# Retention output of a Perceiver block as three one-pass products, its weights split on GpSimd

## The reference

```
x = x + cross_attention(layernorm(x), context)           # 16 heads of 16, masked keys
n = layernorm(x)
q, k, v, g = n @ Wq.T, n @ Wk.T, n @ Wv.T, n @ Wg.T      # retention: 4 heads, q and k 64 wide, v and g 128
q, k = rotary(q), rotary(k)
o = ((q k^T / 8) * decay) @ v                            # causal, decay gamma^(i-j) for each head
o = o * rsqrt(mean(o*o) + 1e-5) * gnorm_w * silu(g)
x = x + o.reshape(256, 512) @ Wo.T                       # "retention output"
m = layernorm(x)
w = softmax(m @ gate_w + gate_b); w = w * (w >= 0.1); w = w / sum(w)
x = x + sum_e w[:, e] * (m @ expert_w[e] + expert_b[e])  # 8 experts
```

## Time and profile before

| | |
|---|---|
| median of 3 runs | 205.86 us (205.49 to 207.44) |
| profiled execution | 204.96 us, span 203.1 us |
| TensorE busy | 193.9 us, 95% of the span, 2446 matmuls |
| VectorE busy | 140.0 us, 69%, 269 instructions |
| ScalarE busy | 108.2 us, 53% |
| GpSimd busy | 74.7 us, 37%, 96 instructions |
| mean granted TensorE clock | 0.995 |

### The profile page before, as it was taken

One profiled execution on the slowest core, in us unless ns is written; L12 is line 12 of the kernel. 1 busy time (PEld: TensorE's weight loads), 2 busy tenths in 40 slices (PEclk: granted clock), 3 DMA queues, 4 the chain that ended last, 5 costly groups with the idle time before them and its releaser, 6 DMA issues.

```text
span 203.1 us, 5924 instructions
## 1 busy us (share of the span) xinstructions
PE 193.9 (95%) x2446; PEld 134.5 (66%) x2446; DVE 140.0 (69%) x269; ACT 108.2 (53%) x230; POOL 74.7 (37%) x96
## 2 busy tenths in 40 slices
PE   8998999989999999999999999999999999999991
PEld 8566654555576767666666656476777888878780
DVE  3482568997388286688888627289676485996893
ACT  3136575759588386788888996244416333201200
POOL 8506695556191241079998331001003013010000
PEclk9999999999999999999999999999999999999998
DMA  5969966338209679066000000000000000000011
GB/s 165 299 189 258 329 161 162 90 85 230 50 5 241 135 207 362 20 217 204 5 5 5 3 0 3 0 3 0 0 0 2 3 0 2 0 5 26 26 32 36
DMA packets 15828, 18.10 MB, mean 89 GB/s; under 512 B 2657, under 2 KB 14897, under 8 KB 15793
## 3 DMA queue, kind: packets, MB, share of 16 engines
q1 hardware_dynamic: 14496, 17.30, 29.1%
q10 hardware_dynamic: 1296, 0.34, 0.8%
HBM read 9.81 MB, written 0.52 MB: 51 GB/s over the span
## 4 chain that ended last, share of the span: by engine, by line
PE 79%; DVE 8%; SPq 4%; ACT 3%; issue 2%; DMA 1%; POOL 0%; DVEq 0%; ACTq 0%; POOLq 0%
PE bank L919 11%; PE bank L1014 11%; PE bank L996 11%; PE bank L876 5%; PE bank L862 4%; DVE cneg L1849 4%; PE bank L1214 3%; PE bank L1064 3%; PE bank L1103 3%; PE bank L1238 3%; PE bank L1107 3%; PE bank L1240 3%; PE bank L1239 3%; PE bank L809 3%; PE bank L1104 3%
## 5 line engine op out<-in xcount | busy, mean ns | idle before, releaser
L1849 DVE TENSOR_REDUCE cneg<-bank 128x1 f32<-128x896 f32 x64 | 67.9, 1088 | 25.1 <-PE bank L919 24.8
L1526 ACT ACTIVATE prob<-bank 128x512 f32<-128x512 f32 x112 | 64.3, 600 | 13.2 <-PE bank L996 11.8
L996 PE MATMUL bank<-qstack,kstack 100*32 100x256 bf16 x896 | 45.0, 273 | 0.8 <-ACT prob L1526 0.5
L919 PE MATMUL bank<-kstack,qstack 97*32 97x448 bf16 x512 | 37.5, 354 | 1.6 <-DVE cneg L1849 0.9
L996 PEld LDWEIGHTS bank<-qstack,kstack 100*32 100x32 bf16 x896 | 24.4, 95 | 18.9 <-ACT prob L1526 4.1
L1014 PE MATMUL bank<-prob,vals 128*32 128x256 f32 x448 | 35.6, 381 | 0.0
L604 POOL TENSOR_TENSOR nw<-nw,halves 128x2 f32<-128x2 f32 (+1 forms) x10 | 8.3, 825 | 63.6 <-DVE nw L1730 45.1
L919 PEld LDWEIGHTS bank<-kstack,qstack 97*32 97x32 bf16 x512 | 13.6, 96 | 7.7 <-DVE cneg L1849 3.5
L1014 PEld LDWEIGHTS bank<-prob,vals 128*32 128x32 f32 x448 | 13.5, 109 | 4.5 <-issue 2.9
L1238 PE MATMUL bank<-exp_high,xn_high 128*128 128x512 f32 (+1 forms) x36 | 14.3, 397 | 0.0
L2095 DVE SCALAR_TENSOR_TENSOR x_in<-bank,nwts,x_in 128x256 f32<-128x256 f32 x28 | 13.5, 482 | 0.8
(11 more groups left out here) (186 smaller groups left out, 322.1 us busy)
## 6 DMA issues: line engine op xcount, KB each, us to landing
kstack<-kpart SPq DMA_DIRECT2D x21, 224.0 KB
w_late<-in_w_ret SPq DMA_DIRECT2D x1, 1536.0 KB, 8.7
mask_all<-in_mask SPq DMA_DIRECT2D x2, 512.0 KB, 4.5
ctxT<-in_w_exp SPq DMA_DIRECT2D x1, 1024.0 KB, 5.3
kpart<-in_w_exp SPq DMA_DIRECT2D x1, 1024.0 KB, 8.9
ctxT<-in_ctxT SPq DMA_DIRECT2D x2, 448.0 KB, 5.0
ctxT<-in_ctxT SPq DMA_DIRECT2D x1, 896.0 KB, 7.9
qstack<-acc SPq DMA_DIRECT2D x12, 64.0 KB, 4.1
```

Of the source, the lines that this page charges most:

```text
L919: mm = pe.matmul(out[j4:j4 + COLS, :], qstack[0:MROW + 1, h, b, qt * P + j4:qt * P + j4 + COLS], kstack[0:MROW + 1, b, h, half_ * HC:(half ...
L996: mm = pe.matmul(out[j4:j4 + COLS, hh * NQ:(hh + 1) * NQ], kstack[0:KROWS, b, h, kt * P + j4:kt * P + j4 + COLS], qstack[0:KROWS, h, b, :] ...
L1526: act.activation(prob[:, n % PROBS, :], bank[:, c.score_bank(u, jj), :], ACT.Exp).then_inc(c["prob_ready"], 1)
L1849: dve.tensor_reduce(cneg[:, st % 2, i:i + 1], bank[:, pair:pair + 2, 0:HC], AXXY, ALU.max, negate=True).then_inc(c["max_read"], 1)
```

## The change

`retention_out` becomes split products. A tile has 12 one-pass matmuls in place of 4 float32 ones: y_high x reto_high and y_high x reto_low, and, once DVE has written the low part, y_low x reto_high. ScalarE's copy writes `y_high` (rounded) and counts on `high_taken`; DVE's new `take_low_y` computes y_low = bank x norm weights - y_high, 128x512, four times. In the first batch these stand after each of the first two decay weights, in the second batch before and after the second of the weight parts' calls. GpSimd cuts `w_reto` in `late_roots`, after the roots of the first two streams, when the second batch's stream is normalised (`n2_ready`): one copy and one subtraction of 128x1024. `y_high` and `reto_high` lie where the second batch's keys were, `y_low` in the room of `y_tok`. `high_taken` now counts y as well, so its waits are indexed by a list. The first batch's biases go one pair of experts later on TensorE, and one step later on DVE.

```
@@ gpsimd, late_roots
                     root(NB + n, width, first)
+                    if n == 1:
+                        pool.wait_ge(s["n2_ready"], TT)
+                        pool.tensor_copy(reto_high[:, :, :], w_reto[:, :, :]).then_inc(s["split"], 1)
+                        pool.wait_ge(s["split"], SPLIT_ALL + 1)
+                        pool.tensor_tensor(reto_low[:, :, :], w_reto[:, :, :], reto_high[:, :, :].bitcast(F32), ALU.subtract).then_inc(s["split"], 1)
+                        pool.wait_ge(s["split"], SPLIT_OUT)
@@ tensor
                 def retention_out(t):
-                    taken("y", t)
+                    pe.wait_ge(s["split"], SPLIT_OUT)
+                    pe.wait_ge(s["high_taken"], HIGH_AT["y", t] + 1)
                     pe.wait_ge(s["rope_read"], TT)
                     out = side("ro", t)
                     for c in range(4):
-                        mm = pe.matmul(out[:, 0:D], yT[:, c, t * P:(t + 1) * P], w_reto[:, c, :], start=(c == 0), stop=(c == 3))
+                        pe.matmul(out[:, 0:D], y_high[:, c, t * P:(t + 1) * P], reto_high[:, c, :], start=(c == 0), stop=False)
+                        pe.matmul(out[:, 0:D], y_high[:, c, t * P:(t + 1) * P], reto_low[:, c, :], start=False, stop=False)
+                    taken("y", t)
+                    for c in range(4):
+                        mm = pe.matmul(out[:, 0:D], y_low[:, t, c, :], reto_high[:, c, :], start=False, stop=(c == 3))
                     mm.then_inc(s["side_ready"], 1)
...
                 pair(1, 0)
+                pair(1, 1)
                 biases(0)
-                pair(1, 1)
                 pair(1, 2)
@@ scalar
                 def take_y(t):
-                    take_turn("y", t, yT[:, :, t * P:(t + 1) * P], bank[:, turn_bank("y", t), :].rearrange("p (f q) -> p f q", f=4), scale=gn[:, 0:1])
+                    assert TURNS[len(takes)] == ("y", t)
+                    act.wait_ge(s["turned"], len(takes) + 1)
+                    act.activation(y_high[:, :, t * P:(t + 1) * P], bank[:, turn_bank("y", t), :].rearrange("p (f q) -> p f q", f=4), ACT.Copy,
+                                   scale=gn[:, 0:1]).then_inc(s["high_taken"], 1)
+                    takes.append(("y", t))
@@ vector
+            def take_low_y(t):
+
+                dve.wait_ge(s["high_taken"], HIGH_AT["y", t] + 1)
+                dve.scalar_tensor_tensor(y_low[:, t, :, :], bank[:, turn_bank("y", t), :].rearrange("p (f q) -> p f q", f=4), gn[:, 0:1],
+                                         y_high[:, :, t * P:(t + 1) * P].bitcast(F32), ALU.mult, ALU.subtract).then_inc(s["turn_taken"], 1)
...
                 decay_weights(RH)
+                take_low_y(0)
                 decay_weights(RH + 1)
+                take_low_y(1)
                 second_stream(0, [lambda: decay_weights(RH + 2)])
...
                 gate_weights(0)
+                take_low_y(2)
                 weight_parts(0)
+                take_low_y(3)
                 add_experts(0, range(0, 6))
                 second_stream(1, [lambda e=e: add_experts(1, [e]) for e in (0, 1)], lambda: add_experts(0, range(6, NE)))
+                add_experts(1, range(2, 4))
                 add_biases(0)
-                add_experts(1, range(2, 4))
                 take_low("n3", 2)
```

More of the change, by code:

```diff
@@ L137 @@
 SPLIT_ALL = 14
+SPLIT_OUT = 16
+KSTACK_BYTES = NB * NH * CH * 2
 PER = {"k_ready": 8, "k_hi": 4, "k_rest": 4, "k_taken": 4, "k_mid": 4, "k_cut": 4, "v_ready": NVP + 2, "v_evac": NVP + 2,
@@ L156 @@
 TURN_AT = {what: n for n, what in enumerate(TURNS)}
+HIGH_AT = {what: n for n, what in enumerate(what for what in TURNS if what[0] in ("n2", "n3", "y"))}
 SIDE_AT = {what: n for n, what in enumerate(SIDES)}
@@ L379, in build @@
         xn_low = sb_over("k_full", 0, "xn_low", [P, KIN, TT * P])
+        reto_high = sb_over("kstack", KSTACK_BYTES - 4 * NV * D // P, "reto_high", [P, NV // P, D])
+        reto_low = sb_over("w_late", 4 * ret_cols, "reto_low", [P, NV // P, D])
+        y_high = sb_over("kstack", KSTACK_BYTES // NB + 4 * 2048, "y_high", [P, NV // P, TT * P])
+        y_low = sb_over("vals", 4 * 1024, "y_low", [P, TT, NV // P, P])
         late0 = qstack[:, :, :, :].rearrange("p h b q -> p (h b q)").bitcast(F32)
@@ L390, in build @@
         qkT = late1[:, 0:4 * TT * P].rearrange("p (f t) -> p f t", f=4)
-        yT = late1[:, 2048:4096].rearrange("p (f t) -> p f t", f=4)
         qk_rot = late1[:, 4096:5120].rearrange("p (t c) -> p t c", t=2)
@@ L1096, in project_ret @@
             def project_ret(t, m, halves=(0, 1)):
-                pe.wait_ge(s["high_taken"], t + 1)
+                pe.wait_ge(s["high_taken"], HIGH_AT["n2", t] + 1)
                 if t:
@@ L1949, in take_low @@
             def take_low(kind, t):
-                n = t + 1 + (TT if kind == "n3" else 0)
-                dve.wait_ge(s["high_taken"], n)
+                dve.wait_ge(s["high_taken"], HIGH_AT[kind, t] + 1)
                 dve.tensor_tensor(xn_low[:, :, t * P:(t + 1) * P], bank[:, turn_bank(kind, t), 0:D].rearrange("p (f q) -> p f q", f=KIN),
                                   xn_high[:, :, t * P:(t + 1) * P].bitcast(F32), ALU.subtract).then_inc(s["turn_taken"], 1)
+            def take_low_y(t):
+                dve.wait_ge(s["high_taken"], HIGH_AT["y", t] + 1)
+                dve.scalar_tensor_tensor(y_low[:, t, :, :], bank[:, turn_bank("y", t), :].rearrange("p (f q) -> p f q", f=4), gn[:, 0:1],
+                                         y_high[:, :, t * P:(t + 1) * P].bitcast(F32), ALU.mult, ALU.subtract).then_inc(s["turn_taken"], 1)
             def first_stream(b):
```

## The result

The changed kernel takes 209.09 us (median of four runs, 207.38 to 210.41) against 205.9 for the kernel before. The ratio is 1.015, with a 95% interval of 1.0077 to 1.0223. The forecast was 208.2 with a range of 205.3 to 209.0, so the sign and the mechanism held, and the median lies 0.09 over the range.

The account below looks back on a forecast made before the run. TensorE, busy 95% of the span, was taken as the bound, with DVE also short of slack in the second batch. Terms -0.61 + 0.81 + 2.1 = +2.3 us gave 208.2 us against the 205.86 median, range 205.3 to 209.0.

Parts of the forecast that it names:

- The products: Retention output on TensorE: one-pass matmuls save 0.61 us per two-tile batch, 1.22 in all; first batch keeps its gain.
- The second batch: Two new DVE instructions add 1.38 us without slack; TensorE's second 0.61 saving goes and gate logits start 0.81 us late.
- The two waits: Second batch: TensorE waits before the third n3 tile's transpose and before its logits, each 0.6 to 0.8 us.
- The biases: First batch's bias product one pair later on TensorE: costs nothing, waiting under 0.1 us instead of over 1 us.
- GpSimd's split: After the second stream is normalised: GpSimd's subtraction starts 0.3 us before DVE's rotation, costing between 0 and 2.1 us.
- the upper end: At DVE's first rotation: it starts only when GpSimd's subtraction is over, a loss of 2.1 us; taken for the forecast.
- The rival of full speed: Rotation loses nothing beside GpSimd's subtraction, or DVE comes first: +0.2 us, 206.1; chance 0.30.
- sharing: At the rotation, DVE is slowed beside GpSimd, not stopped: half of 2.1 us, +1.25 in all, 207.1; chance 0.12.
- the rival of the hidden DVE work: Second batch's low parts take under 0.57 us, logits not late, no rotation loss: 205.25 or 204.6; chance 0.07.
- the products are not one pass: Retention output matmuls run at the old 0.217 us, 1.7 us more in the first batch: 209.7; chance 0.03.
- The sum: Whole kernel: -0.61 first batch, +0.81 second batch, +2.1 rotation, giving +2.3 us and 208.2 us.
- no clock effect enters: Retention output stretches: granted clock is 1.00 in both, the 2.4 GHz level, so no time was added for it.

Follow-up runs that it names:

- the reordered kernel: Changed kernel with GpSimd's copy and subtraction held until the third tile is rotated, plus DVE's second-batch expert sums in another order; 205.2 us, ratio 0.9954.
- the two halves: Changed kernel with GpSimd's subtraction issued as two instructions of 512 elements instead of one; 209.03 us in a single run.
- the split alone: Kernel before plus only GpSimd's new copy and subtraction at the change's place, results unread; 208.72 us, ratio 1.0136.

## Why the prediction was right, and where it fell short

**The products.** 0.61 a batch was predicted; the first batch gave 0.59 in the trace of after, and 0.60 in the tail of the kernel that has it alone. The reading that the low parts come in time, and that DVE then waits less for the product (0.79 instead of 1.30), held.

**The second batch.** The loss was put at 0.81 and is 0.96. The two waits are where they were said to be, each 0.54 to 0.55 where 0.6 to 0.8 was said. The low part's instruction was priced by the gate product's 0.69 and is booked with 0.74 to 0.75, but the next one starts before it is over: the two move what stands behind them by 1.42 (the last of the gate weights starts 2.70 later than before, 176.44 against 173.74, the first expert sum 4.12, 178.38 against 174.26), where 1.38 was said. That is 0.04 of the 0.15; another 0.06 is the step from the low part's end to the logits, 0.11 where 0.05 was said. That DVE's list, and not the amount of its work, sets this loss is shown by the reordered kernel.

**The biases.** It was said that their move costs nothing, and the two traces show nothing: 61.73 with either place.

**GpSimd's split.** This was the choice that decided: between 0 and 2.1 the upper end was taken, from rows that showed no such pair side by side, chiefly the 4.00 us in which GpSimd stood off from DVE's products. That row is a wait written into GpSimd's list, so it shows how the kernel is written and not what the engines do; the choice was right, but no measurement stood behind it. It is 1.93. The start of GpSimd's work, and so the lead of 0.3 us, came as estimated. The 0.2 of difference is that the held instruction ends 0.28 after the subtraction and not a whole 0.42: what the hold adds is a little less than what was left of the subtraction. TensorE's weight load for the low part waits 2.36, where 2.5 was said. The rival of full speed is refuted by three kernels (2.36, 2.35, 2.38), sharing by the two halves (1.28 and 1.48, in turns), the rival of the hidden DVE work by the two waits, and that the products are not one pass by the 0.59.

**The sum.** -0.59 + 0.96 + 1.93 = +2.30, and +2.3 was said. That it fits so closely is luck: 0.15 too little in the second batch and 0.17 too much at the rotation cancel.

**What was missed.** The step that failed is in the first paragraph of the prediction: the granted clock was 1.00, "so no clock effect enters". That was so before, where TensorE had no long wait; the change makes one of 1.92 us. Where a trace shows a fall of the clock, in the two halves, it stands right behind that wait; that half of the runs of after have one there is read from their mean clocks alone. The four runs of after are 207.38 and 208.76 at clocks of 0.998 and 0.999, and 209.43 and 210.41 at 0.988 and 0.989: means of 208.07 and 209.92, 1.85 apart, with the forecast of 208.2 at the first of them. The mean of the four is 209.0. As far as two runs tell, the sum of the terms was right for a run at the full clock; the median lies between the two kinds of run.

## What to carry to other kernels

Work on an idle engine isn't free because it is idle: before GpSimd is given something that reads SBUF, look at which DVE instructions with two SBUF operands will start while it runs, and move the wait that lets it go until none of them is on the path (one condition was worth 2.0 us of tail here). A one-pass product that saves TensorE time and hands a low part to another engine pays only where that engine still waits for TensorE; where it doesn't, first look for an instruction in its list that can go later, since some 1.2 us came back from order alone. And a new wait of TensorE should be priced twice: once for its length, and once for the clock behind it.

## What the runs showed of the hardware

- The held DVE instruction is booked as busy: 2.36, 2.35 and 2.38 us instead of 0.42, with no releaser named. A duration that is several times the usual one for its shape is the sign, and the chain's "issue" of 2.24 beside it.
- The clock after a wait of TensorE of 1.92 us fell to 0.50 in some executions and not in others: in four of six runs with the split alone and two of four of after by their mean clocks, in the profiled execution of the two halves (a tail of 69.25 where after has 67.71), and in neither profiled execution of after and of the split alone. What decides between them wasn't found.
- Ahead of the change's place, in the attention, the same instructions took up to 2.45 us longer from one profiled execution to another (the variance starts between 137.84 and 140.29). The stop of TensorE at 76 us, 1.19 to 1.21 us long, stands in three of the ten. In these three a packet of the DMA queue q8, an instruction queue by the page, moved between 74.7 and 75.8; in the other seven it moved between 71.0 and 73.0. That the one causes the other was not tested.
